# A two-layer conditioned transformer on one core: two orders of work per attention unit, on ScalarE and on VectorE, are swapped

## The chip, the cores and the metric

One Trainium2 chip, of which the kernel uses one core. The metric is the time of one execution on the device in microseconds (us), of which the median over several runs counts. The engines of the core are TensorE (PE in the profile, its weight loads PEld), VectorE (DVE), ScalarE (ACT), GpSimd (POOL) and SyncE (SP), which issues every DMA of this kernel.

## What is computed

Input are 16 sequences of 256 tokens with 512 features, float32. Two transformer layers follow each other:

```
layer 0: h = layernorm(x) * (1 + scale) + shift
         q = h Wq (16 heads of 32), latent = h Wkd, k = latent Wku, v = latent Wvu (4 kv heads)
         rotate q, k;  softmax(q k / sqrt(32), window of 64 and every 64th key, by blocks of 128) v
         x = x + y Wo
layer 1: h = rmsnorm(x) * gain1;  q = h Wq (8 heads of 64), k = h Wk, v = h Wv (one kv head)
         rotate q, k;  softmax(q k / sqrt(64), all 256 keys) v;  x = x + y Wo
         h = rmsnorm(x) * gain2;  x = x + (silu(h Wg) * (h Wu)) Wd        (inner width 2048)
```

The matrix products are made of float16 halves: each operand is a high half (the value rounded to float16) and a low half (the rest), and a product is three matmuls, high by high, high by low and low by high.

## The kernel before, in words

**Rounds.** The 16 sequences go in 8 pairs. The attention of both layers of pair n runs together with the MLP of pair n-1: a round. The first round has no MLP beside it (it prepares the weights instead), seven rounds are a loop with both, and a last MLP stands alone. A table `PLAN` of named steps (`scores0`, `unit0_0` to `unit0_23`, `unit1_0` to `unit1_15` and others) says how many of the MLP's 128 parts, of six 128x512 matmuls each for the first 64, TensorE makes at each step. A chunk of the MLP is four parts: two for the gate bank, two for the up bank.

**Units.** A unit is one PSUM bank of scores: four heads by 128 keys (layer 0, first 128 tokens, units 0 to 7), two heads by 193 keys (layer 0, last 128 tokens, units 8 to 23) or two heads by 256 keys (layer 1, 16 units). For each unit j:

1. TensorE makes the scores (`unit_scores`, L1403 in layer 0, L1407 and L1409 in layer 1). It does so two units ahead (`AHEAD = 2`): at step j it makes the parts of the MLP, the scores of unit j+2, then the values of unit j-4 (`LAG = 4`).
2. VectorE takes the minimum of each head's row (`lows`, L1027 with the mask in layer 0, L1031 in layer 1).
3. ScalarE takes the exponentials in place, a head at a time, with their sums (`exps`, L808).
4. ScalarE writes the float16 high half into `prob` (`prob_highs`, L817). `prob` has three slots, so this waits for the transposition of unit j-3 (`turned_before`), and for the exponentials of its own unit (`terms_made`).
5. VectorE writes the low half (`prob_lows`, L1038). This frees the bank.
6. SyncE transposes both halves by DMA into `prob_t` (`turn_probs`, L563; the fifth place of the ring is named `x_mid` or `q_t`), once the values of unit j-5 are made.
7. TensorE multiplies with v (`unit_values`, L1339 to L1341 with `v_hi`, `v_lo`).

There are four banks for the scores (`BANKS = 4`), used in a fixed order. The scores of unit j+2 wait in `bank_for` for the `prob_lows` of the bank's last user, unit j-2 as a rule.

**What else stands in the units' steps.** ScalarE has two hooks for the MLP: `ahead(step)` makes the tanh of a chunk whose gate products fall in this step (`tanhs`, L970, waits for TensorE), `behind(step)` the high half of a finished chunk (`inner_highs`, L976). VectorE's `between` makes the gate's product (`gates`, L1296, waits for the tanh) and the chunk's inner value (`inners`, L1306). SyncE loads the next weights of the MLP, 512 KB at a time, at the step that finishes a chunk (`ring_loads`, L542), in the one queue that also has the transpositions. Every engine runs its own list in order; only semaphores tie them.

Of the kernel before, what the change touches and what calls it, by code (L numbers as in the profile page):

```python
# [100 lines left out]
def unit_index(layer, j):  # L101
    return layer * UNITS[0] + j
# [87 lines left out]
def chunks_at(step, done):  # L190
    return [f for f in range(FCH) if 4 * f + done - 1 in parts_at(step)]
# [6 lines left out]
def count(n, per, k):  # L198
    i, off = n
    return off * per + k if i is None else i * per + (off * per + k)  # L200


def need(eng, sem, value):
    if isinstance(value, int) and value <= 0:
        return
    eng.wait_ge(sem, value)
# [20 lines left out]
def build(nc, x, cond_t, pos_t, w_ada_t, b_ada_t, wq0_t, wkd_t, wku_t, wvu_t, wo0_t, ln1_w, tw1_t,  # L227
          ln2_w, tw2_t, wq1_t, wk1_t, wv1_t, wo1_t, wg_t, wu_t, wd_t, mask_c, rope0_c, freq_c,
          wgu, out):
    with ExitStack() as ctx:  # L230
# [232 lines left out]
        def terms(ap, layer, j):  # L463
            s, t, columns = UNIT[layer][j]
            if columns[0][2] != K_TWO:
                return ap
            return ap.rearrange("p (h k) -> p h k", k=TOK)[:, :, 0:K_TWO]
# [11 lines left out]
        def turned_before(eng, n, g):  # L479

            if g < SLOTS:
                n, last = (n[0], n[1] - 1), max(k for k in range(sum(UNITS))
                                                if k % SLOTS == g % SLOTS)
            else:
                last = g - SLOTS
            need(eng, prob_in[last % TURNED], turned_count(n, last))
# [288 lines left out]
        def _(act):  # L775
# [18 lines left out]
            def heads(n, layer, s, t):  # L794
                use = USE[f"heads{layer}", s, t]
                need(act, full, count(n, USES, use + 1))
                act.activation(act_t[s][0][:, :, t * P:(t + 1) * P],
                               work_bank[use % BANKS][:].rearrange("p (c q) -> p c q", c=CH),
                               ACT.Copy).then_inc(hi_done, 1)
# [13 lines left out]
            def prob_highs(n, layer, j):  # L813
                g = unit_index(layer, j)
                need(act, terms_made, count(n, sum(UNITS), g + 1))
                turned_before(act, n, g)
                act.activation(terms(prob[:, g % SLOTS, 0, :], layer, j),  # L817
                               terms(work_bank[USE[f"unit{layer}", j] % BANKS][:], layer, j),
                               ACT.Copy).then_inc(hi_done, 1)

            def layers(n, m):
                def ahead(step):
                    if m is not None:
                        tanhs(m, chunks_at(step, 2))
                    else:
                        weight_highs(step)
                        if step == "fill2.0":
                            act.wait_ge(gains_made, 4 * CH)
                    if step == SINES_AT:
                        sines_((n[0], n[1] + 1))  # L830

                def behind(step):
                    if m is not None:
                        inner_highs(m, chunks_at(step, 4))
# [6 lines left out]
                def units(layer):  # L841
                    total = UNITS[layer]
                    ahead(f"scores{layer}")
                    exps(n, layer, 0)
                    behind(f"scores{layer}")
                    for j in range(total):
                        if j + 1 < total:
                            exps(n, layer, j + 1)
                        ahead(f"unit{layer}_{j}")
                        prob_highs(n, layer, j)  # L850
                        if j in FILL_AT[layer]:
                            heads(n, layer, FILL_AT[layer][j], 0)
                        behind(f"unit{layer}_{j}")
# [100 lines left out]
            def weight_highs(step):  # L954
                for piece in PIECES_AT.get(step, ()):
                    act.wait_ge(*landed[PIECE_OF[piece][0]])
                    for src, dst in piece_views(piece, 0):
                        ins = act.activation(dst, src, ACT.Copy, scale=WS)
                    ins.then_inc(raw_high, 1)

            def sines_(n):
                need(act, angle_ready, count(n, 1, 1))
                act.activation(reduced, reduced, ACT.Sin).then_inc(sines, 1)

            def tanhs(n, chunks):
                for f in chunks:
                    need(act, g_full, count(n, FCH, f + 1))
                    if f > 0:
                        need(act, inner_ready, count(n, FCH, f))
                    act.activation(silu[:], gbank[:], ACT.Tanh, scale=0.5 / WS).then_inc(  # L970
                        tanh_done, 1)
# [18 lines left out]
        def _(dve):  # L990
# [44 lines left out]
            def prob_lows(n, layer, j):  # L1035
                name, slot = (f"unit{layer}", j), unit_index(layer, j) % SLOTS
                need(dve, hi_done, count(n, HI_USES, HI_USE[name] + 1))
                dve.tensor_tensor(terms(prob[:, slot, 1, :], layer, j),  # L1038
                                  terms(work_bank[USE[name] % BANKS][:], layer, j),
                                  terms(prob[:, slot, 0, :], layer, j),  # L1040
                                  ALU.subtract).then_inc(prob_split, 1)
# [16 lines left out]
            def units(n, m, layer):  # L1058
                total = UNITS[layer]
                between(m, f"scores{layer}")  # L1060
                lows(n, layer, 0)
                lows(n, layer, 1)
                for j in range(total):
                    step = f"unit{layer}_{j}"
                    between(m, step)
                    if step in LN_STATS:
                        ln_stats((n[0], n[1] + 1), LN_STATS[step])
                    elif step in LN_APPLY:
                        ln_apply((n[0], n[1] + 1), LN_APPLY[step])
                    if j + 2 < total:  # L1070
                        lows(n, layer, j + 2)
                    prob_lows(n, layer, j)
                    if j in FILL_AT[layer]:
                        heads_low(n, layer, FILL_AT[layer][j], 0)
                    if j in NORM_AT[layer]:
                        normalise(n, layer, NORM_AT[layer][j], 0)
# [60 lines left out]
            def ln_apply(n, s):  # L1137
                need(dve, ln_rstd_ready, count(n, 2, s + 1))
                for t in range(TILES):
                    dve.tensor_scalar(normed[s][:, t, :], x_in[:, s, t, :], moments[:, s, t, 0:1],  # L1140
                                      ln_rstd[:, s, t:t + 1], ALU.subtract, ALU.mult).then_inc(
                                          ln_ready, 1)
# [550 lines left out]
```

## Time and profile before

| | |
|---|---|
| median of three runs | 1889.67 us (1888.66 to 1891.92) |
| the profiled execution's own time | 1891.67 us |
| its span | 1889.9 us |
| TensorE busy | 1733.3 us, 92% |
| VectorE busy | 1162.3 us, 61% |
| ScalarE busy | 928.2 us, 49% |
| GpSimd busy | 380.4 us, 20% |
| mean granted TensorE clock | 0.965 of full speed |

A busy time is a union over instructions. Matmuls overlap, so a TensorE that is busy 92% of the span is not one that streams at its peak for 92% of it. The idle time that a view gives before an instruction is the time in which its engine had nothing running, and the releaser is what ended it.

### The profile page before, as it was taken

To read this page: it belongs to the slowest core of one execution; us is meant where nothing else is said; L and a number is where in the kernel's file an instruction comes from. 1 tells how busy PE (TensorE), PEld (TensorE's weight loads), DVE (VectorE), ACT (ScalarE), POOL (GpSimd) and SP (SyncE) were. 2 spreads that over 40 slices of the span, in tenths; PEclk is the share of its full clock that TensorE was granted. 3 is DMA by queue.
4 is the path that set the end of the run, shared out by engine and by line. 5 is a ranking of instruction groups with operands and counts; after the bars stand their busy time and mean duration, and the time that the engine had idled before them with its cause. 6 is when DMAs were issued, how large, how long until landed. Compare 5 with 4: busy or idle time off the path is not lost.

```text
span 1889.9 us, 38576 instructions
## 1 busy us (share of the span) xinstructions
PE 1733.3 (92%) x12496; PEld 953.7 (50%) x12496; DVE 1162.3 (61%) x2960; ACT 928.2 (49%) x2783; POOL 380.4 (20%) x530
## 2 busy tenths in 40 slices
PE   6656799999999999899999999999999999999999
PEld 4533444555455554455445554555545554455444
DVE  5758657574576756676576755766576755767320
ACT  3644537454473546545374545635465444735320
POOL 5847511111110111111111111102111101111120
PEclk9567799999999999999999999999999999999999
DMA  7996439552594527843495616925286535946220
GB/s 241 223 287 181 89 87 182 127 110 77 131 177 93 107 76 167 148 104 73 126 177 121 123 58 140 194 73 101 89 182 132 116 81 126 175 100 118 89 73 23
DMA packets 520638, 240.86 MB, mean 127 GB/s; under 512 B 476368, under 2 KB 485584, under 8 KB 520400
## 3 DMA queue, kind: packets, MB, share of 16 engines
q1 hardware_dynamic: 520400, 238.01, 57.1%
q8 instruction: 110, 1.80, 0.4%
q14 instruction: 128, 1.05, 0.2%
HBM read 96.38 MB, written 16.78 MB: 60 GB/s over the span
## 4 chain that ended last, share of the span: by engine, by line
PE 71%; DMA 10%; DVE 8%; issue 4%; ACT 4%; SPq 2%; DVEq 0%; POOL 0%; ACTq 0%; POOLq 0%
DMA prob_t<-prob 10%; PE up L1339 7%; PE gate L1341 7%; PE gate L1339 7%; PE up L1341 7%; PE gate L1340 7%; PE up L1340 7%; PE bank L1339 4%; PE bank L1340 4%; PE bank L1341 4%; PE y L1339 4%; PE y L1340 3%; PE y L1341 3%; PE bank L1366 2%; ACT bank L808 2%
## 5 line engine op out<-in xcount | busy, mean ns | idle before, releaser
L808 ACT ACTIVATE bank<-bank,low 128x128 f32<-128x128 f32 (+2 forms) x768 | 304.3, 399 | 162.9 <-DVE low L1031 106.0
L680 POOL TENSOR_TENSOR inner_t<-inner,inner_t 128x512 f16<-128x512 f32 x128 | 148.0, 1156 | 792.5 <-ACT inner_t L976 792.5
L1038 DVE TENSOR_TENSOR prob<-bank,prob 128x512 f16<-128x512 f32 (+1 forms) x320 | 203.7, 637 | 100.9 <-ACT prob L817 99.9
L817 ACT ACTIVATE prob<-bank 128x512 f16<-128x512 f32 (+1 forms) x320 | 180.9, 565 | 58.6 <-DMA prob_t<-prob 53.5
L1296 DVE SCALAR_TENSOR_TENSOR silu<-silu,gate 128x512 f32<-128x512 f32 x128 | 87.9, 687 | 186.3 <-ACT silu L970 186.3
L1339 PE MATMUL up<-mlp,ring 128*128 128x512 f16 x512 | 194.5, 380 | 0.7 <-DVE inner L1306 0.7
L1339 PE MATMUL gate<-mlp,ring 128*128 128x512 f16 x512 | 194.1, 379 | 0.4 <-DVE mlp L1007 0.4
L1341 PE MATMUL gate<-mlp,ring 128*128 128x512 f16 x512 | 194.4, 380 | 0.0
L1340 PE MATMUL gate<-mlp,ring 128*128 128x512 f16 x512 | 194.2, 379 | 0.0
L1341 PE MATMUL up<-mlp,ring 128*128 128x512 f16 x512 | 194.2, 379 | 0.0
L1340 PE MATMUL up<-mlp,ring 128*128 128x512 f16 x512 | 194.2, 379 | 0.0
L808 ACT ACTIVATION_READ_ACCUMULATOR bank<-bank,low 128x1 f32 x768 | 160.9, 210 | 0.0
L1027 DVE CUSTOM_DVE_ANT_0 bank<-bank,mask 128x193 f32<-128x193 f32 (+1 forms) x512 | 152.5, 351 | 4.0 <-PE bank L1403 3.9
L1339 PE MATMUL y<-v_hi,prob_t 128*128 128x32 f16 (+2 forms) x1024 | 111.6, 187 | 35.3 <-DMA prob_t<-prob 34.4
L1306 DVE SCALAR_TENSOR_TENSOR inner<-up,silu 128x512 f32<-128x512 f32 x128 | 87.9, 687 | 79.7 <-PE up L1341 79.0
L970 ACT ACTIVATE silu<-gate 128x512 f32<-128x512 f32 x128 | 76.8, 600 | 115.3 <-PE gate L1341 114.3
L951 ACT ACTIVATE work<-x_mid 128x512 f32<-128x512 f32 x64 | 40.3, 630 | 177.1 <-DVE x_mid L1096 177.1
L976 ACT ACTIVATE inner_t<-inner 128x512 f16<-128x512 f32 x128 | 80.7, 630 | 77.9 <-DVE inner L1306 77.9
L1339 PEld LDWEIGHTS y<-v_hi,prob_t 128*128 128x128 f16 (+1 forms) x1024 | 91.2, 99 | 50.1 <-DMA prob_t<-prob 42.8
L1339 PE MATMUL y<-wq_hi,act_hi 128*128 128x512 f16 x256 | 98.2, 384 | 13.5 <-DVE work L1103 12.0
L1340 PE MATMUL y<-v_lo,prob_t 128*128 128x32 f16 (+2 forms) x1024 | 110.2, 185 | 0.0
L1341 PE MATMUL y<-v_hi,prob_t 128*128 128x32 f16 (+2 forms) x1024 | 110.1, 185 | 0.0
(168 smaller groups left out, 4047.2 us busy)
## 6 DMA issues: line engine op xcount, KB each, us to landing
ring<-wgu_dram SPq DMA_DIRECT2D x124, 512.0 KB, 3.9
x_in<-x_dram SPq DMA_DIRECT2D x18, 512.0 KB, 5.4
x_res<-x_mid SPq DMA_DIRECT2D x16, 512.0 KB, 3.0
out_dram<-x_res SPq DMA_DIRECT2D x32, 256.0 KB, 2.3
inner_t<-wg_t_dram SPq DMA_DIRECT2D x8, 512.0 KB, 5.2
inner_t<-wu_t_dram SPq DMA_DIRECT2D x8, 512.0 KB, 5.1
prob_t<-prob SPq DMA_TRANSPOSE x256, 3.3
wgu_dram<-ring SPq DMA_DIRECT2D x8, 512.0 KB, 5.1
```

The source lines that it names most:

```text
L680: pool.tensor_tensor(inner_t[:, 1, f, :], inner[:], inner_t[:, 0, f, :], ALU.subtract).then_inc(inner_low, 1)
L808: ins = act.activation(bank_[:, at:at + wid], bank_[:, at:at + wid], ACT.Exp, bias=low[:, j % BANKS, k:k + 1], scale=-1.0, accum_out=total)
L817: act.activation(terms(prob[:, g % SLOTS, 0, :], layer, j), terms(work_bank[USE[f"unit{layer}", j] % BANKS][:], layer, j), ACT.Copy).then_ ...
L970: act.activation(silu[:], gbank[:], ACT.Tanh, scale=0.5 / WS).then_inc(tanh_done, 1)
L976: act.activation(inner_t[:, 0, f, :], inner[:], ACT.Copy).then_inc(inner_high, 1)
L1027: ins = dve.tensor_tensor_reduce(out=view, in0=view, in1=mask[:, 0:wid], scale=1.0, scalar=3.0e38, op0=ALU.add, op1=ALU.min, accum_out=low ...
L1038: dve.tensor_tensor(terms(prob[:, slot, 1, :], layer, j), terms(work_bank[USE[name] % BANKS][:], layer, j), terms(prob[:, slot, 0, :], lay ...
L1296: dve.scalar_tensor_tensor(silu[:], silu[:], 1.0, gbank[:], ALU.add, ALU.mult).then_inc(gated, 1)
L1306: dve.scalar_tensor_tensor(inner[:], ubank[:], 0.5 * HS / (WS * WS), silu[:], ALU.mult, ALU.mult).then_inc(inner_ready, 1)
L1339: pe.matmul(out_ap, left[0], right[0], start=start, stop=False)
L1340: pe.matmul(out_ap, left[0], right[1], start=False, stop=False)
L1341: return pe.matmul(out_ap, left[1], right[0], start=False, stop=stop)
```

## The change

Two swaps, nothing else. On ScalarE, `prob_highs` of unit j stood behind the exponentials of unit j+1 and the tanh of the step; it now stands ahead of both, and the exponentials stand behind the tanh. On VectorE, `prob_lows` of unit j stood behind `lows` of unit j+2; it now stands ahead.

```diff
@@ units(layer), ScalarE
                     for j in range(total):
+                        prob_highs(n, layer, j)
+                        ahead(f"unit{layer}_{j}")
                         if j + 1 < total:
                             exps(n, layer, j + 1)
-                        ahead(f"unit{layer}_{j}")
-                        prob_highs(n, layer, j)
                         if j in FILL_AT[layer]:
                             heads(n, layer, FILL_AT[layer][j], 0)
                         behind(f"unit{layer}_{j}")
@@ units(n, m, layer), VectorE
+                    prob_lows(n, layer, j)
                     if j + 2 < total:
                         lows(n, layer, j + 2)
-                    prob_lows(n, layer, j)
                     if j in FILL_AT[layer]:
                         heads_low(n, layer, FILL_AT[layer][j], 0)
```

No instruction is added or taken away, and nothing on TensorE, GpSimd or SyncE moves in its own list.

How the instructions stand on ScalarE in the loop, layer 0, from unit 8's exponentials (bank2, 193 columns) on, before:

```order
L808 ACTIVATE bank2,sums0<-bank2,low 128x193 x2
L817 ACTIVATE prob<-bank1 128x512
L206 REGISTER_ALU
L808 ACTIVATE bank3,sums0<-bank3,low 128x193 x2
L206 REGISTER_ALU
L817 ACTIVATE prob<-bank2 128x2x193
L206 REGISTER_ALU
L808 ACTIVATE bank0,sums0<-bank0,low 128x193 x2
L817 ACTIVATE prob<-bank3 128x2x193
L976 ACTIVATE inner_t<-inner 128x512
```

And the same place in the changed kernel:

```order
L808 ACTIVATE bank2,sums0<-bank2,low 128x193 x2
L206 REGISTER_ALU
L817 ACTIVATE prob<-bank2 128x2x193
L206 REGISTER_ALU
L808 ACTIVATE bank3,sums0<-bank3,low 128x193 x2
L817 ACTIVATE prob<-bank3 128x2x193
L206 REGISTER_ALU
L808 ACTIVATE bank0,sums0<-bank0,low 128x193 x2
L976 ACTIVATE inner_t<-inner 128x512
L817 ACTIVATE prob<-bank0 128x2x193
```

Before, a bank's high half comes one unit's exponentials after its own; now it comes right behind them, with only a hook of the MLP (L976) between in some steps.

VectorE at step `unit0_0` of the loop, before (unit 2's minima in bank0, unit 0's low half from bank2):

```order
L1296 SCALAR_TENSOR_TENSOR silu<-silu,gate 128x512
L213 REGISTER_ALU
L1027 ISA bank0,low<-bank0,mask 128x128
L1027 ISA low 128x1
L1027 ISA bank0,low<-bank0,mask 128x128
L1027 ISA low 128x1
L1027 ISA bank0,low<-bank0,mask 128x128
L1027 ISA low 128x1
L1027 ISA bank0,low<-bank0,mask 128x128
L1027 ISA low 128x1
L206 REGISTER_ALU
L1038 TENSOR_TENSOR prob<-bank2,prob 128x512
```

And now:

```order
L1296 SCALAR_TENSOR_TENSOR silu<-silu,gate 128x512
L206 REGISTER_ALU
L1038 TENSOR_TENSOR prob<-bank2,prob 128x512
L213 REGISTER_ALU
L1027 ISA bank0,low<-bank0,mask 128x128
L1027 ISA low 128x1
L1027 ISA bank0,low<-bank0,mask 128x128
L1027 ISA low 128x1
L1027 ISA bank0,low<-bank0,mask 128x128
L1027 ISA low 128x1
L1027 ISA bank0,low<-bank0,mask 128x128
L1027 ISA low 128x1
```

The low half moved in front of the whole of the minima; the gate's product, which waits for the tanh, still stands ahead of both.

## Rows read from the trace of the kernel before

**Rows 1.** The page: busy time by engine, and TensorE in 40 slices

```profile
PE 1733.3 (92%) x12496; PEld 953.7 (50%) x12496; DVE 1162.3 (61%) x2960; ACT 928.2 (49%) x2783; POOL 380.4 (20%) x530
PE   6656799999999999899999999999999999999999
```

**Rows 2.** TensorE's waits, 240 to 1740 us (the seven rounds): us, times, longest

```profile
PE y L1339 <- DMA prob_t<-prob: 22.4, 28, 2.2
PE bank L1403 <- DVE prob L1038: 16.1, 21, 1.2
```

**Rows 3.** TensorE's waits, 0 to 240 us (the first round)

```profile
PE bank L1407 <- DVE prob L1038: 14.9, 9, 2.8
PE y L1339 <- DMA prob_t<-prob: 12.0, 11, 1.9
PE bank L1403 <- DVE prob L1038: 9.3, 13, 0.9
```

**Rows 4.** Timeline of TensorE at three places: start, us, instruction, idle before

```profile
957.76 0.40 PE L1403 MATMUL bank<-k_t,q_t 96*128 96x128 f16 x4 [1.23 <-DVE prob L1038]
...
999.93 0.34 PE L1403 MATMUL bank<-k_t,q_t 96*128 96x193 f16 x2 [0.71 <-DVE prob L1038]
...
1176.22 0.28 PE L1403 MATMUL bank<-k_t,q_t 96*128 96x128 f16 x2 [1.22 <-DVE prob L1038]
```

**Rows 5.** Timeline of VectorE, 955 to 957 us

```profile
955.46 0.69 DVE L1296 SCALAR_TENSOR_TENSOR silu<-silu,gate 128x512 f32<-128x512 f32 x1 [2.30 <-ACT silu L970]
956.06 0.29 DVE L1027 CUSTOM_DVE_ANT_0 bank<-bank,mask 128x128 f32<-128x128 f32 x1
...
957.01 0.69 DVE L1038 TENSOR_TENSOR prob<-bank,prob 128x512 f16<-128x512 f32 x1
```

**Rows 6.** Timeline of ScalarE, 954 to 959 us

```profile
954.82 0.60 ACT L970 ACTIVATE silu<-gate 128x512 f32<-128x512 f32 x1 [1.46 <-PE gate L1341]
955.32 0.59 ACT L817 ACTIVATE prob<-bank 128x512 f16<-128x512 f32 x1
...
957.19 0.34 ACT L808 ACTIVATE bank<-bank,low 128x128 f32<-128x128 f32 x1 [0.76 <-DVE low L1027]
...
957.55 0.33 ACT L808 ACTIVATE bank<-bank,low 128x128 f32<-128x128 f32 x1
...
958.58 0.61 ACT L817 ACTIVATE prob<-bank 128x512 f16<-128x512 f32 x1
```

**Rows 7.** Timeline of VectorE, 969 to 971 and 998 to 1000 us

```profile
969.60 0.36 DVE L1027 CUSTOM_DVE_ANT_0 bank<-bank,mask 128x193 f32<-128x193 f32 x1
...
970.19 0.69 DVE L1038 TENSOR_TENSOR prob<-bank,prob 128x512 f16<-128x512 f32 x1
...
998.72 0.36 DVE L1027 CUSTOM_DVE_ANT_0 bank<-bank,mask 128x193 f32<-128x193 f32 x1
...
999.31 0.56 DVE L1038 TENSOR_TENSOR prob<-bank,prob 128x386 f16<-128x386 f32 x1
```

**Rows 8.** Timeline of SyncE's queue and, last, of TensorE, 969 to 977 us

```profile
969.04 0.45 SPq L542 DMA_DIRECT2D ring<-wgu_dram  x1
970.95 5.20 SPq L563 DMA_TRANSPOSE prob_t<-prob  x3
...
976.07 0.19 PE L1339 MATMUL y<-v_hi,prob_t 128*128 128x32 f16 x1 [1.27 <-DMA prob_t<-prob]
```

**Rows 9.** DMA of one round's layer 0 units, 946 to 1008 us: KB each, median us to landing

```profile
ring<-wgu_dram SPq DMA_DIRECT2D x9, 512.0 KB, 3.9
prob_t<-prob SPq DMA_TRANSPOSE x20, 4.0
```

**Rows 10.** Windows: one layer 0 units' stage, the first round's layer 1 (last: clock, DMA share, GB/s)

```profile
946.00:1008.00 62.00, 56.53 (x520) 30.90 (x519) 44.81 (x173) 45.70 (x171) 11.10 (x10) 1.00 0.95 184
168.00:212.00 44.00, 26.12 (x228) 18.76 (x229) 34.87 (x57) 27.16 (x87) 31.63 (x44) 0.54 0.71 141
```

**Rows 11.** ScalarE's waits, 240 to 1740 us

```profile
ACT silu L970 <- PE gate L1341: 94.9, 42, 5.2
...
ACT prob L817 <- DMA prob_t<-prob: 34.1, 34, 3.6
```

**Rows 12.** VectorE's waits, 168 to 212 us (the first round's layer 1)

```profile
DVE prob L1038 <- ACT prob L817: 4.2, 7, 1.3
```

**Rows 13.** Timeline of VectorE, 978.8 to 980 us (the second waits for the first)

```profile
978.83 0.24 DVE L1082 RECIPROCAL inv<-sums 128x16 f32<-128x16 f32 x1
979.10 0.69 DVE L1084 TENSOR_TENSOR work<-y,inv 128x512 f32<-128x512 f32 x1
979.71 0.68 DVE L1296 SCALAR_TENSOR_TENSOR silu<-silu,gate 128x512 f32<-128x512 f32 x1
```

## The prediction

> **What bounds the kernel now.** I read the page first: TensorE is busy 92% of the span and, once the first round is over at about 240 us, nine tenths or more of nearly every slice [rows 1]. So a change that moves no matmul can win only what TensorE idles. I then asked for TensorE's waits, apart for the seven rounds of the loop and for the first. In the loop two releasers can be touched by this change: a unit's transposition that lands late (22.4 us in 28 waits) and a low half that frees a bank of scores late (16.1 us in 21) [rows 2]. That is 38.5 us in seven rounds, 5.5 us a round. In the first round the same two kinds come to 36.2 us [rows 3], but there ScalarE, VectorE and the DMA queue set the pace and TensorE has little to do, so a wait of TensorE there is a symptom.
>
> The third view is the timeline of the round that ends near 1165 us. There the 1.23 us before the scores at 957.76 end with a low half [rows 4]. That low half, of unit 1, stood behind the masked minima of unit 3: VectorE's minima began at 956.06 and the low half at 957.01 [rows 5]. Its input, the high half, was made at 955.32 to 955.91 [rows 6]. So it could have begun at 956.06.
>
> **The change part by part.** The durations are those of the profiled execution, whose time is 1891.67 us, 2.0 above the median of the three runs; I take the difference from the median.
>
> *The scores' waits.* Three gaps of this kind come back in every round (21 waits in seven rounds). The low half now starts before the minima, so it comes earlier by what the minima take: 0.95 us at the first (956.06 to 957.01) [rows 5], 0.59 at the second (969.60 to 970.19) and 0.59 at the third (998.72 to 999.31) [rows 7]. The first gap is 1.23 us, the third 0.71 [rows 4]; the second must be 16.1 / 7 - 1.23 - 0.71 = 0.36 us, less than its 0.59. I take 0.95 + 0.36 + 0.59 = 1.9 us a round. Bounds: nothing, if each low half now waits for something else, and all 2.3 us.
>
> *The transpositions' waits.* A high half now comes earlier on ScalarE: at the tanh of 954.82 [rows 6] the list was exponentials 2, tanh 1, high 1, and unit 2's high half had to wait for exponentials 3, until 958.58. Now, after the tanh's 0.50 us (954.82 to 955.32), exponentials 2 take four times 0.35 (957.19 to 958.58 for four), and high half 2 follows at about 956.9, or 957.4 with L976 between. So it is 1.2 to 1.7 us earlier, and VectorE's low half follows it without the minima between. The transposition is issued when both are there. How much of that reaches the landing? Transposition 6, which TensorE waited 1.27 us for, was issued at 970.95 and landed at about 976.0: 5.1 us, because a load of 512 KB was issued at 969.04, just ahead of it in the same queue [rows 8]. The load, in turn, had waited on SyncE behind the transposition of unit 5, which waits for that unit's low half. Both move forward, but TensorE moves forward too when the scores' waits go, so a landing must come earlier by that much to keep its gap as it is. I take half of the 22.4 us, 1.6 us a round. Bounds: nothing and 3.2 us.
>
> *Behind the tanh.* The exponentials of unit j+1 now stand behind the tanh of step j, which waits for TensorE's gate products (94.9 us in 42 waits) [rows 11]. They lose the head start they had. I cost this at nothing: a tanh at T leaves high half j+1 done at about T + 0.5 + 1.4 + 0.6 = T + 2.5, where before it was T + 0.5 + 0.6 + 1.4 + 0.6 or later, with exponentials j+2 in front. The cover is that ScalarE has 16.3 us idle in these 62 us and VectorE 17.2 [rows 10]. Minima j+2 come later by a low half, 0.6 us, but exponentials j+2 are not wanted before high half j+1 is done.
>
> *The wait for its own engine.* The high half used to have another unit's exponentials between it and its own, and now waits for the instruction right before it. The nearest row is VectorE's reciprocal, at 978.83 for 0.24 us, with its user starting at 979.10, 0.03 us after the end, where instructions that don't wait start 0.08 us before the end (979.71 after one that ends at 979.79) [rows 13]. So 0.11 us a unit, 40 units a round. In the loop ScalarE's idle time covers it. In the first round's units 0 to 7 ScalarE is the pace, and 8 x 0.11 is 0.9 us; the end of that stretch is set by the transpositions, so I count 0 with a bound of +2. The Trainium skill, VectorE: DVE Perf Modes, section The DRAIN you can't avoid, says that a semaphore after each copy costs nothing extra over a chain without. By it this term would be zero everywhere; rows 13 show a small cost, and the sum is the same by both.
>
> *The first round.* In its layer 0 the transpositions share the queue with the weights' loads; earlier halves change nothing there: 0, bounds -3 and +2. In its layer 1 VectorE is busy 34.9 of 44 us [rows 10] and waits 4.2 us for high halves that stood behind exponentials [rows 12]. I take 3 us of that; bounds 0 and 9, the latter if waits of PE's chain behind it go too.
>
> Sum: 7 x (1.9 + 1.6) = 24.5, plus 3: 27.5 us. 1889.7 - 27.5 is **1862 us**. With all waits of rows 2 gone and the far bounds of the first round it is 38.5 + 9 + 3 = 50.5, 1839 us.
>
> **The rivals.**
>
> *A. The DMA queue is already the limit in layer 0's units.* For: the DMA engines' share is 0.95 over 62 us [rows 10], and a transposition takes 4.0 us to land at the median there [rows 9]. Then the order of the engines is of no use beyond the earlier start. Each round would win about the first 0.95 us, the first round 3: 1889.7 - 6.7 - 3 = 1880 us. Against: SyncE issues three transpositions in 5.2 us right behind a load [rows 8], 1.7 us each, against some 2.6 us a unit in the stage (62 us / 24), and with 9 loads in the stage there is a little room. The Trainium skill, DMA: Bandwidth & Descriptors, section Latency and other measured facts, gives 261 GB/s as the effective rate of one transposing kernel; 256 KB of `prob` are an estimated 1.0 us by it. The stage moves 184 GB/s [rows 10], so by that page too rival A would be the less likely.
>
> *B. The tanh behind the high half (slower).* The high half j waits for the transposition of unit j-3 (34.1 us in 34 waits, 3.6 the longest, in the loop) [rows 11], and the tanh of step j is now behind it. The gate bank then is free late, and TensorE's next gate products wait. TensorE has 12 up matmuls of about 0.22 us in between, 2.6 us; tanh and gate product take 0.60 + 0.69 [rows 5, 6]. So it decides from a wait of 1.3 us on. If all 34.1 us fell before a tanh that TensorE needs, and only the 1.9 us a round were won, it would be 34.1 - 13.3 = +21: 1911 us. Against: the tanh stands in one step of three or so, most of these waits are under 1.3 us (mean 1.0), and a tanh that does not wait comes earlier by up to a unit's exponentials.
>
> *C. Nothing (same).* The waits for transpositions grow by what the waits for banks shrink, since both lists are tied to TensorE through gate and scores: within 3.8 us of 1889.7, say 1888.
>
> **How the numbers follow.** My forecast has 0.52, rival A 0.24, C 0.13, B 0.11. A measurement of this kernel tells about 0.2% (3.8 us) from no change. A's 1880 is faster by more than that; a small part of it may end within. So faster 0.76, within 0.2% 0.13, slower 0.11. The range goes down to 1843, near the far bound of the sum, and up to 1889, which takes in A and part of C, and leaves out B.
>
> **What would show it.** In the changed profile the three waits of TensorE's L1403 for VectorE's L1038 in each round should be two, shorter ones or none, near 3 us in total in place of 16.1; its waits for transpositions should be about 11 us in the loop. ScalarE's idle time before L817 should end with DMA oftener than now, and VectorE's wait for L817 in the first round's layer 1 should fall from 4.2 to about 1 us. A round, now 218.5 us from this wait to the same wait of the next (957.76 to 1176.22) [rows 4], should be about 215. I am wrong if TensorE waits for `silu` at gate products (B), if its waits for transpositions stay at 22 us or grow (A, C), or if the busy time of any engine changes.

## The result, and the profile after

The changed kernel takes **1873.16 us**, the median of four runs (1872.47 to 1873.19), against 1890.67 us for four runs of the kernel before (1888.66 to 1891.92). The ratio is 0.9907, 95% interval 0.9891 to 0.9922: 17.5 us faster, where 27.5 were forecast. The profiled execution took 1873.14 us, its span is 1871.3, and I compare it with the span of 1889.9 before: 18.6 us.

Where did they come from? The starts of the rounds, taken at the same instruction of ScalarE in the two traces, stand 2.5 us earlier at the end of the first round and 16.2 us earlier six rounds later, where the eighth round begins; the span is 18.6 us shorter. So a round is about 2.3 us shorter (13.7 us in six), and all behind the first round, the last MLP included, 16.1.

The page of the changed kernel, beside [rows 1]. Of the 18.6 us, 13.6 are less idle time of TensorE (156.6 us before, 143.0 now) and 5.0 less busy time, which no view explains:

```profile
PE 1728.3 (92%) x12496; PEld 951.8 (51%) x12496; DVE 1157.8 (62%) x2960; ACT 944.5 (50%) x2783; POOL 381.1 (20%) x530
PE   6656799999989999899999999999999999999999
```

TensorE's waits from 240 to 1740 us, beside [rows 2] (us, times, longest):

```profile
PE y L1339 <- DMA prob_t<-prob: 11.5, 16, 1.3
PE y L1339 <- DVE work L1084: 9.3, 14, 0.7
PE bank L1403 <- issue: 8.2, 7, 1.5
PE bank L1403 <- DVE prob L1038: 6.2, 14, 0.7
PE up L1339 <- DVE inner L1306: 6.1, 9, 0.8
```

The two waits that the change was aimed at fell from 22.4 and 16.1 us to 11.5 and 6.2: 20.8 us. But two others grew, which I had not named: the wait for the normalised rows (L1084) was 3.8 us in 7 waits before and is 9.3 in 14, the wait of the `up` product for the MLP's inner (L1306) was 0.7 in 2 and is 6.1 in 9. They give 10.9 us back. With the issue wait (9.6 before) these waits shrink by 11.3 us. All idle time of TensorE from 240 to 1740 us fell by 12.1 us (1432.6 us busy of 1500 before, 1444.7 now), so next to nothing of the gain lies in idle times that this view leaves out; what is missing to the 16.1 us is busy time.

In the first round, 0 to 240 us, beside [rows 3]:

```profile
PE bank L1407 <- DVE prob L1038: 13.0, 8, 2.8
PE y L1339 <- DMA prob_t<-prob: 11.6, 11, 1.7
PE bank L1403 <- DVE prob L1038: 9.9, 13, 1.4
```

The timeline of TensorE in one round (start, us, instruction, idle before), beside [rows 4]. The first place has 0.27 us where it had 1.23, the second none, the third (here in the round after) still 0.72. New are the gaps before `up` and before the value products at 966.86 and 969.52:

```profile
946.80 0.40 PE L1403 MATMUL bank<-k_t,q_t 96*128 96x128 f16 x4 [0.27 <-DVE prob L1038]
...
952.34 0.39 PE L1339 MATMUL up<-mlp,ring 128*128 128x512 f16 x1 [0.74 <-DVE inner L1306]
...
966.86 0.19 PE L1339 MATMUL y<-v_hi,prob_t 128*128 128x32 f16 x1 [0.93 <-DMA prob_t<-prob]
...
969.52 0.19 PE L1339 MATMUL y<-v_hi,prob_t 128*128 128x32 f16 x1 [0.73 <-DVE work L1084]
...
1203.68 0.34 PE L1403 MATMUL bank<-k_t,q_t 96*128 96x193 f16 x2 [0.72 <-DVE prob L1038]
```

Who made `up` wait at 952.34? VectorE's inner L1306, whose bank `up` needs. Here is VectorE's list up to it, changed and then before:

```profile
945.46 0.69 DVE L1296 SCALAR_TENSOR_TENSOR silu<-silu,gate 128x512 f32<-128x512 f32 x1 [1.47 <-ACT silu L970]
...
950.04 0.69 DVE L1038 TENSOR_TENSOR prob<-bank,prob 128x512 f16<-128x512 f32 x1 [0.48 <-ACT prob L817]
950.64 0.29 DVE L1027 CUSTOM_DVE_ANT_0 bank<-bank,mask 128x128 f32<-128x128 f32 x1
...
951.60 0.69 DVE L1306 SCALAR_TENSOR_TENSOR inner<-up,silu 128x512 f32<-128x512 f32 x1
```

```profile
959.22 0.69 DVE L1038 TENSOR_TENSOR prob<-bank,prob 128x512 f16<-128x512 f32 x1 [0.51 <-ACT prob L817]
...
961.10 0.69 DVE L1038 TENSOR_TENSOR prob<-bank,prob 128x512 f16<-128x512 f32 x1 [0.18 <-ACT prob L817]
961.71 0.68 DVE L1306 SCALAR_TENSOR_TENSOR inner<-up,silu 128x512 f32<-128x512 f32 x1
```

VectorE waited for high halves in this stretch before as well (0.51 and 0.18 us), so the low half's wait of 0.48 us is not new. What changed is how the engines stand to each other. Against the kernel before, the gate's product starts 10.00 us earlier (955.46, now 945.46), the scores of the first place 10.96 (957.76, now 946.80), and the inner 10.11 (961.71, now 951.60). Between the gate's product and the inner VectorE has the same work in either order: the low halves come sooner, the minima later, the inner hardly moves. So TensorE, let go 0.96 us sooner at the scores, comes to `up` before the inner is made and starts it 10.11 us earlier (962.45 before). It keeps 0.11 us of the 0.96. These steps are the same within 0.02 us in all seven rounds, and in a second profile of the changed kernel.

At 969.52 TensorE waits for the normalised rows. VectorE and ScalarE around it, now:

```profile
967.42 0.56 DVE L1038 TENSOR_TENSOR prob<-bank,prob 128x386 f16<-128x386 f32 x1 [1.85 <-ACT prob L817]
...
968.77 0.69 DVE L1084 TENSOR_TENSOR work<-y,inv 128x512 f32<-128x512 f32 x1
```

```profile
966.89 0.50 ACT L817 ACTIVATE prob<-bank 128x386 f16<-128x386 f32 x1 [1.46 <-DMA prob_t<-prob]
```

Read upwards: the value product waits for the rows of 968.77, these stand behind a low half that waited 1.85 us for a high half, and that one had waited 1.46 us for a transposition to read a `prob` buffer. Such a chain was there before, too, one low half sooner in the list:

```profile
976.64 0.56 DVE L1038 TENSOR_TENSOR prob<-bank,prob 128x386 f16<-128x386 f32 x1 [1.83 <-ACT prob L817]
```

The rows came at 979.10 then [rows 13], and TensorE hardly waited for them (0.07 us, at 979.85). They now come 10.33 us earlier. TensorE was further ahead than that at the product before (977.85, now 966.86: 10.99 us), so it had to wait.

The third place of [rows 4], on VectorE, beside the last pair of [rows 7]:

```profile
1201.40 0.56 DVE L1038 TENSOR_TENSOR prob<-bank,prob 128x386 f16<-128x386 f32 x1
...
1202.46 0.69 DVE L1306 SCALAR_TENSOR_TENSOR inner<-up,silu 128x512 f32<-128x512 f32 x1
1203.07 0.56 DVE L1038 TENSOR_TENSOR prob<-bank,prob 128x386 f16<-128x386 f32 x1
```

The minima are gone from right ahead of this low half, but the inner stands there (before, it stood ahead of the minima), and its high half was itself only done at 1202.82. Of the 0.59 us counted for this place, some 0.1 came (0.61 us mean of seven gaps now, 0.70 before).

The stage of the layer 0 units and the DMA issues in it, 934 to 996 us, beside [rows 9, 10]:

```profile
934.00:996.00 62.00, 58.43 (x531) 32.01 (x531) 46.03 (x176) 48.13 (x174) 11.57 (x10) 1.00 0.95 192
```

```profile
prob_t<-prob SPq DMA_TRANSPOSE x20, 3.4
```

TensorE is busy 58.4 us of 62 where it was 56.5, at the same DMA share of 0.95 (57.1 us at 0.98 in the second profile, 930 to 992 us). So the share was no wall. That transpositions land sooner is not shown: the median of these 20 is 3.4 us where it was 4.0, but 3.8 in the second profile, and over the 224 of the loop it is 3.3 us where it was 3.2.

ScalarE's and VectorE's waits that answer to [rows 11] and [rows 12], the loop and then the first round's layer 1:

```profile
ACT silu L970 <- PE gate L1341: 110.3, 56, 5.2
...
ACT prob L817 <- DMA prob_t<-prob: 42.3, 31, 4.3
```

```profile
DVE prob L1038 <- ACT prob L817: 1.1, 1, 1.1
```

### The profile page after: what moved, and what is told of

It reads as the page before. It is cut to its first block, busy times and chain, and to the rows that moved or that the text cites. A ratio compares the mean times of both kernels' runs of the same rounds, so it can differ in the third digit from the quotient of the medians.

```text
span 1871.3 us, 38576 instructions
## 1 busy us (share of the span) xinstructions
PE 1728.3 (92%) x12496; PEld 951.8 (51%) x12496; DVE 1157.8 (62%) x2960; ACT 944.5 (50%) x2783; POOL 381.1 (20%) x530
## 4 chain that ended last, share of the span: by engine, by line
PE 71%; DMA 9%; DVE 8%; ACT 5%; issue 4%; SPq 2%; DVEq 0%; POOL 0%; ACTq 0%; POOLq 0%
DMA prob_t<-prob 8%; PE gate L1341 7%; PE gate L1339 7%; PE gate L1340 7%; PE up L1339 7%; PE up L1341 7%; PE up L1340 7%; PE bank L1339 4%; PE bank L1340 4%; PE bank L1341 4%; PE y L1339 4%; PE y L1341 4%; PE y L1340 4%; ACT bank L808 3%; PE bank L1366 2%
## 5 line engine op out<-in xcount | busy, mean ns | idle before, releaser
L1306 DVE SCALAR_TENSOR_TENSOR inner<-up,silu 128x512 f32<-128x512 f32 x128 | 88.1, 689 | 82.2 <-PE up L1341 75.1
L976 ACT ACTIVATE inner_t<-inner 128x512 f16<-128x512 f32 x128 | 81.2, 634 | 77.9 <-DVE inner L1306 77.9
L1339 PE MATMUL y<-wq_hi,act_hi 128*128 128x512 f16 x256 | 98.7, 386 | 11.3 <-DVE work L1103 10.3
```

The costliest lines, as they stand in the source:

```text
L976: act.activation(inner_t[:, 0, f, :], inner[:], ACT.Copy).then_inc(inner_high, 1)
L1306: dve.scalar_tensor_tensor(inner[:], ubank[:], 0.5 * HS / (WS * WS), silu[:], ALU.mult, ALU.mult).then_inc(inner_ready, 1)
L1339: pe.matmul(out_ap, left[0], right[0], start=start, stop=False)
```

## The experiments

**Theory:** each half of the change takes away what it was meant to, and the size is cut by other feeds of TensorE that VectorE makes no sooner than before. **Rivals:** the place of the tanh is what matters, in either direction (B); the DMA queue is the limit (A); one of the two swaps does it all. The kernel before took 1893.5 to 1895.8 us at the median beside these runs, and 1890.67 in the first comparison, so each run is given as a ratio to the kernel before beside it, on the same chip. A wait is read from one profile of each run.

### One swap at a time

`act_only`: the changed kernel with VectorE's list as before.

```diff
-                    prob_lows(n, layer, j)
                     if j + 2 < total:
                         lows(n, layer, j + 2)
+                    prob_lows(n, layer, j)
```

> The swap on ScalarE alone, VectorE in its old order. Theory (each swap has its own part): the low half is made behind the minima as before, so TensorE's waits for banks (L1403 for L1038, 16.1 us before and 6.2 in the changed kernel, 240 to 1740 us) stay at 12 to 16 us, while its waits for transpositions (22.4 before, 11.5 changed) fall most of the way; time about 1880 us. Rival (ScalarE's swap is all of it): 1873 us as the changed kernel, and bank waits near 6 us.

Measured: 1887.74 us, ratio 0.9965 (0.9951 to 0.998). In the loop TensorE's waits are

```profile
PE bank L1403 <- DVE prob L1038: 19.0, 28, 1.2
PE y L1339 <- DMA prob_t<-prob: 17.4, 23, 1.7
...
PE y L1339 <- DVE work L1084: 3.8, 7, 0.5
```

`dve_only`: ScalarE's list as before, VectorE's as changed.

```diff
-                        prob_highs(n, layer, j)
-                        ahead(f"unit{layer}_{j}")
                         if j + 1 < total:
                             exps(n, layer, j + 1)
+                        ahead(f"unit{layer}_{j}")
+                        prob_highs(n, layer, j)
```

> The swap on VectorE alone, ScalarE in its old order. Theory (the two swaps need each other): low half j now waits in front of minima j+2, while high half j still stands behind exponentials j+1, and exponentials j+2 need minima j+2; ScalarE and VectorE take turns. A 193-column unit then takes 0.8 (exponentials) + 0.42 (high) + 0.5 (low) + 0.65 (minima) + about 0.2 = 2.6 us against some 2.0 that TensorE needs, a 256-column unit 0.9 + 0.5 + 0.6 + 0.6 + 0.2 = 2.8 against 2.3: over 7 rounds 16 x 0.6 x 7 + 16 x 0.5 x 7 = 120 us more, about 2010 us (1930 to 2090). Rival (each swap has its own part): the bank waits go and it is 1880 us.

Measured: 2089.53 us, ratio 1.1042 (1.101 to 1.1075): 195 us more, where the sum said 120. In the loop, first VectorE's wait, then ScalarE's:

```profile
DVE prob L1038 <- ACT prob L817: 204.8, 167, 2.1
```

```profile
ACT bank L808 <- DVE low L1027: 173.8, 138, 1.8
```

What follows: the halves don't add up. Alone, ScalarE's swap wins over a third of the gain (0.35%). TensorE's waits for transpositions fall by 5 us, but those for the scores' banks rise from 16.1 to 19.0, and the wait for L1084 (3.8) stays; of the 4.3 us by which its span is shorter than that of the kernel before, 3.0 lie in the first round. VectorE's swap alone costs 10%: its minima for unit j+2 stand behind low half j, which waits for a high half that stands behind exponentials j+1, so the two engines take turns (204.8 and 173.8 us, where the kernel before has 72.7 and 54.8). Some 54 of the 198 us by which its span is longer are busy time of TensorE (1786.9 us), whose granted clock was 0.97 to 0.98 in the loop and not 0.99 to 1.00; the sum had no entry for that. Only with the high half moved does the low half have an input when its turn comes. The scores' waits fall below 16.1 us only when both halves are there; those for L1084 rise with VectorE's half (11.8 us in `dve_only`).

### The place of the tanh

`tanh_behind` puts the tanh (the `ahead` hook) behind the exponentials, `tanh_first` ahead of the high half, and `old_tanh_first` gives the old order of both engines with the tanh ahead of the exponentials (its diff is against the kernel before).

```diff
                         prob_highs(n, layer, j)
-                        ahead(f"unit{layer}_{j}")
                         if j + 1 < total:
                             exps(n, layer, j + 1)
+                        ahead(f"unit{layer}_{j}")
```

> The changed kernel with the tanh back behind the exponentials of unit j+1 (high j, exponentials j+1, tanh, high of the inner value). Theory (the early high half makes the gain, the tanh's place little): within 4 us of the changed kernel's 1873. Rival (the gain came from the earlier tanh, by which VectorE's gate product and all behind it are earlier): the tanh is 0.8 to 1.4 us later in every step that has one, low halves behind the gate product too, and half of the gain or more is gone: 1882 us or over.

Measured: 1898.21 us, ratio 1.002 (1.0005 to 1.0035). The whole gain is gone, and the theory with it. VectorE waits 183.0 us for the tanh in the loop in place of 139.6, and ScalarE 58.3 us for the masked minima in place of 10.8. TensorE's waits for transpositions are even shorter (8.0 us), but:

```profile
PE bank L1403 <- DVE prob L1038: 15.5, 21, 1.3
PE y L1339 <- DVE work L1084: 12.9, 14, 1.1
```

```diff
-                        prob_highs(n, layer, j)
                         ahead(f"unit{layer}_{j}")
+                        prob_highs(n, layer, j)
                         if j + 1 < total:
                             exps(n, layer, j + 1)
```

> The changed kernel with the tanh ahead of the high half (tanh j, high j, exponentials j+1), VectorE in the new order. Theory (the high half must not wait for TensorE): in the steps with a tanh the high half waits for the gate products, some 2 us on average in 56 waits, and the waits for transpositions rise again from 11.5 to 15 to 20 us in the loop; 4 to 10 us slower than the changed kernel beside it. Rival (what matters is only that the tanh is ahead of the exponentials): within 3 us of it.

Measured: 1882.23 us, ratio 0.9945 (0.9922 to 0.9969), some 8 us slower than the change. The waits for transpositions stayed at 11.6 us, so the cause that was expected isn't it. Its profile shows the inner's waits at 9.5 us (6.1 and 7.4 in two profiles of the changed kernel), a first round at least 4 us longer than theirs, and some 5 us or more behind it. What makes them is open.

```diff
+                        ahead(f"unit{layer}_{j}")
                         if j + 1 < total:
                             exps(n, layer, j + 1)
-                        ahead(f"unit{layer}_{j}")
                         prob_highs(n, layer, j)
```

> The kernel before with one edit: the tanh moved ahead of the exponentials of unit j+1 (tanh j, exponentials j+1, high j), VectorE in its old order. It asks whether the tanh's earlier place alone makes the gain, since with the tanh behind the exponentials the changed order had none. Theory (tanh and high half must both be ahead): the tanh waits for TensorE before the exponentials are begun, and the high half comes behind both, 0.8 to 1.4 us later than before wherever the tanh waits for TensorE; ratio 1.00 to 1.02. Rival (it is the tanh's place alone): ratio 0.990 to 0.994.

Measured: 1901.15 us, ratio 1.0041 (1.002 to 1.0063); one of the ten executions took 6222.86 us, the others 1896.92 to 1906.74. The tanh's earlier place alone wins nothing; the scores' waits rise to 25.2 us. Together: the swap pays only with the tanh ahead of the exponentials, and the tanh there does not pay without the swap.

### The change once more, and its first round

`changed_again` is the changed kernel unchanged, to see what of the profile comes back.

> The changed kernel once more, as the reference for the runs beside it on the same chip: ratio to the kernel before 0.991, as first measured.

Measured: 1874.55 us, ratio 0.9903 (0.9881 to 0.9925); waits for transpositions 11.1, L1084 9.3, inner 7.4, scores 6.5 us. Behind the first round it is 14.4 us shorter than the kernel before (16.1 in the first profile). In the first profile the last exponential of the first round's layer 0 had come 3.5 us later than before (at 124.0 us, not 120.5); here it comes at 120.1. But here that layer's first exponential had come at 57.3 us, where it came at 61.5 in the other two. From first to last exponential the layer takes 62.8 us, and 62.5 in the first profile, against 59.1 before.

`first_old` gives ScalarE, `first_both_old` both engines, the old order in the first round's layer 0 alone.

```diff
+                        if m is None and layer == 0:
+                            if j + 1 < total:
+                                exps(n, layer, j + 1)
+                            ahead(f"unit{layer}_{j}")
+                            prob_highs(n, layer, j)
+                        else:
...
```

> The changed kernel with ScalarE's old order in the first round's layer 0 alone. Between the first round's start and the end of its layer 0 the changed kernel is 3.5 us behind. Theory (ScalarE sets the pace there and pays for waiting on its own exponentials, 0.13 us a unit, and starts in later DMA slots): those 3.5 us come back, 1870 us. Rival (it is how the DMA queue falls, VectorE's order or chance): 1873 us, and the layer still ends some 3 us late.

Measured: 1882.95 us, ratio 0.9943 (0.9924 to 0.9962). The scores' waits of the first round rise to 28.9 us from 9.9. This was a badly made experiment: it left VectorE's new order there, and so shows the coupling of `dve_only` again and nothing of what was asked.

VectorE's part of `first_both_old` (ScalarE's is that of `first_old`):

```diff
+                    old = m is None and layer == 0
+                    if not old:
+                        prob_lows(n, layer, j)
                     if j + 2 < total:
                         lows(n, layer, j + 2)
+                    if old:
+                        prob_lows(n, layer, j)
```

> The changed kernel with the old order of both engines in the first round's layer 0. The run with ScalarE's alone had VectorE's new order beside it there, and TensorE's waits for banks in that stage rose from 9.9 to 28.9 us. Theory: with both old, the 3.5 us by which the changed kernel is late at the end of that layer come back, and 2 to 4 us of the time. Rival (chance of the DMA queue): no difference beyond 1 us.

Measured: 1873.91 us, ratio 0.9906 (0.9876 to 0.9936). Against 1874.55 of the change on the same chip it is no difference. But the interval is 0.3% to either side, some 6 us, and the effect asked for was 2 to 4. In its profile the layer's first exponential comes at 57.7 us and the last at 120.0, 62.3 us with the old order. So the layer ends at 120.0 to 120.1 with either order when it begins at 57 to 58 us, and at 120.5 with the old and 124.0 with the new when it begins at 61.5. Whether the order costs anything there is open.

### What holds back the rest

Four runs on the 10.9 us of new waits, and on the transpositions' 11.5 us. `norm_first`:

```diff
+                    if j in NORM_AT[layer]:
+                        normalise(n, layer, NORM_AT[layer][j], 0)
                     if j + 2 < total:
                         lows(n, layer, j + 2)
...
-                    if j in NORM_AT[layer]:
-                        normalise(n, layer, NORM_AT[layer][j], 0)
```

> The changed kernel with the normalising of attention rows (DVE L1084) put between a unit's low half and the minima of the unit two ahead. Theory (half of what the swap won is given back because VectorE's other work in the unit now stands behind the minima, which wait for newer scores): TensorE's waits for L1084 in 240 to 1740 us fall from 9.3 us to under 4, some other wait grows by at most 2, loop 3 to 6 us shorter than the changed kernel's, ratio to the kernel before 0.986 to 0.989. Rival (the waits named there only take the place of one another, TensorE is held by the sum of the feeds): L1084 falls, L1403 or the inner L1306 rises by as much, ratio 0.990 to 0.992.

Measured: 1880.51 us, ratio 0.9914 (0.99 to 0.9928).

```profile
PE y L1339 <- DMA prob_t<-prob: 17.4, 20, 1.6
...
PE y L1339 <- DVE work L1084: 2.7, 5, 0.5
```

The wait for L1084 fell by 6.6 us as the theory had it, but TensorE's waits for transpositions rose by 5.9. It was the rival that held, though by another wait than the one it named. In the profile a round is 0.5 to 0.7 us longer than in the two of the changed kernel, and the first round 5 to 7 us, so half or more of what it is slower by lies in the first round; in time, the interval takes in the change's 0.9907. `inner_first`:

```diff
                         prob_highs(n, layer, j)
                         ahead(f"unit{layer}_{j}")
+                        behind(f"unit{layer}_{j}")
                         if j + 1 < total:
                             exps(n, layer, j + 1)
...
-                        behind(f"unit{layer}_{j}")
```

> The changed kernel with the inner highs (the hook behind each unit on ScalarE) put ahead of the next unit's exponentials, as the tanh is. Theory (the new waits of the up product for the inner, 6 to 7 us in 240 to 1740, come from the inner's turn on the two engines): these waits fall to under 3, and the exponentials come about 0.4 us later in the units that carry an inner; ratio 0.987 to 0.990. Rival (the inner's low part on VectorE is what is late, since L1306 is VectorE's and stands behind a low half that itself waits for ScalarE): the waits stay at 6 or grow, and the bank's waits grow too, ratio 0.990 to 0.995.

Measured: 1882.27 us, ratio 0.9924 (0.9911 to 0.9937). The inner's waits are 6.2 us, unmoved: they are made on VectorE, as the rival said, and as the starts at 951.60 and 961.71 above show. Putting the inner ahead of the minima on VectorE, which stand right before it now, was not tried. The scores' waits hardly grew (6.9, against 6.2 and 6.5); those for transpositions did, to 14.4. `norm_inner` has both edits.

> Both of the two edits above at once. Theory: the two gains add up, waits for L1084 and L1306 both under 4 us in 240 to 1740, ratio 0.983 to 0.988. Rival (one limit behind both): no better than the better of the two, ratio 0.989 to 0.995.

Measured: 1880.76 us, ratio 0.9917 (0.9899 to 0.9934). No better than either; waits for transpositions 16.3 us, L1084 3.2, inner 6.6. `load_after`:

```diff
-                    ring_loads(m, step, False)
                     turn(n, step)
+                    ring_loads(m, step, False)
```

> The changed kernel with SyncE's ring loads of a step issued behind that step's transposition instead of ahead of it. Theory (the 11 us that TensorE still waits for transpositions are transfers that share the queues with a step's weight loads): DMA waits in 240 to 1740 fall from 11 to 3 to 8 us, and some matmuls wait for weights for 0 to 4 us; ratio 0.985 to 0.990. Rival A of the prediction (the DMA queues are full whatever the order): the waits only move, DMA as a whole 10 to 14 us, ratio 0.990 to 0.993.

Measured: 1892.56 us, ratio 0.9981 (0.997 to 0.9991), nearly the whole gain lost, against both expectations.

```profile
PE y L1339 <- DMA prob_t<-prob: 21.3, 13, 2.9
PE up L1339 <- DVE inner L1306: 16.6, 16, 1.5
```

Fewer waits for transpositions, but longer ones. All that a round is longer by, 2.8 us, lies between the first and the last exponential of layer 0 (59.0 us mean, 56.0 in the changed kernel). SyncE's queue there shows what the load's old place gave. First the changed kernel, then this one:

```profile
956.17 1.23 SPq L563 DMA_TRANSPOSE prob_t<-prob  x1
957.57 0.46 SPq L542 DMA_DIRECT2D ring<-wgu_dram  x1
960.25 5.22 SPq L563 DMA_TRANSPOSE prob_t<-prob  x3
```

```profile
959.47 1.24 SPq L563 DMA_TRANSPOSE prob_t<-prob  x1
960.87 0.45 SPq L542 DMA_DIRECT2D ring<-wgu_dram  x1
961.60 5.22 SPq L563 DMA_TRANSPOSE prob_t<-prob  x2
```

In the changed kernel the load at 957.57 goes out in the 2.7 us in which SyncE has no transposition to issue, and three transpositions follow together. With the load behind its step's transposition, a load (960.87) is issued between transpositions that are ready. ScalarE then waits longer for `prob` buffers: 50.6 us for `prob_t` transpositions in the loop, against 44.8 in `changed_again`, and 20.2 against 7.2 for those into `x_mid`. So a transposition that lands late does not only hold TensorE; through the buffer it delays high half, low half and all behind them.

In `norm_first` and `norm_inner` a wait of TensorE is taken away (L1084) and returns at the next feed (the transpositions). I read it as a ring: a unit's buffer is free when its transposition has landed, the next high half waits for that, its low half for the high half, its transposition for both. A fourth `prob` buffer, which would open this ring, was not tried. That the ring is what limits the stage is thus argued from the waits, not shown. None of the orders tried is faster than the change beyond its interval; `first_both_old`, `norm_first`, `norm_inner` and, just, `inner_first` can't be told from it.

## Why the prediction was right, and where its size was off

The likeliest case came, faster by more than 0.2%, inside the range, at 17.5 us where 27.5 stood. The two waits fell for the reasons given, by nearly the 24.5 us of the sum (20.8), but half of that was given back by feeds that the sum left out.

- *The scores' waits*, 1.9 us a round by the sum: 16.1 to 6.2 us is 1.4. At the first place the gap went from 1.23 to 0.27 us, the 0.95 counted, of which 0.11 was left at the next `up`; the second, 0.36, is gone; the third gave some 0.1 of its 0.59. The step that failed at the third was to take the minima as all that stood ahead of the low half: in the new list the inner L1306 is right in front of it, and its own high half is late. The text looked for near 3 us in total and a round of 215; they are 6.2 us and 216.4.
- *The transpositions' waits*, 1.6 us a round: 22.4 to 11.5 us is 1.56. "Half" was a guess, and it came to half. `act_only` shows 5 of these 10.9 us as coming with ScalarE's half.
- *TensorE's other feeds* were missing. The sum made no entry for feeds that VectorE makes no sooner while TensorE comes sooner: 5.5 us more for L1084 and 5.4 for the inner, 1.6 us a round. For the inner it is shown to the hundredth: of the 0.96 us won at the scores 0.85 are lost again at `up`, in each of seven rounds. This is the term by which the loop's 24.5 us became 16: 20.8 of the two waits, less 10.9, with 1.4 from the issue wait and some 4 in TensorE's busy time. `norm_first` shows that it isn't a cost with a cure of its own: with its wait gone, that for transpositions is 17.4 again. The text had named the mechanism ("TensorE moves forward too") for one kind of wait only.
- *Behind the tanh*, cost 0: TensorE does not wait for `silu` at gate products among its larger waits. That the idle time of both engines was the cover is not shown. The part hides a term as large as the whole gain: `tanh_behind` keeps the swap with exponentials ahead of the tanh, and is 1.1% slower (1.002 against 0.9907). The sum had no entry for what the tanh's earlier place gives, and that it was not missed is in part luck.
- *The wait for its own engine*, 0.11 us a unit: 0.13 to 0.14 measured on ScalarE, below, which the loop covers. The Trainium skill's VectorE: DVE Perf Modes, section The DRAIN you can't avoid, by which the term would be zero, speaks of copies on VectorE; on ScalarE no run shows it at zero.
- *The first round*, 3 us: 2.5 in the first profile, 5.3 in `changed_again`. In layer 1 VectorE's wait for the high half went from 4.2 to 1.1 us as expected, and from first to last exponential the layer takes 34.7 us in both, 36.8 before. Layer 0, put at 0 with a bound of +2, took 3.4 to 3.7 us longer, with the cause open.
- *The signs of being wrong* had "if the busy time of any engine changes", and it did: ScalarE's from 928.2 to 944.5 us, TensorE's from 1733.3 to 1728.3. The sign was a bad one. Busy time is a union, and the high half no longer overlaps the instruction ahead of it, as the last section shows; the instructions are the same.
- *Rival A* gave a round some 0.95 us and waits that stay at 22 us; a round won 2.3, and the waits halved at a DMA share as high as before. *Rival B*'s wait did grow, ScalarE's for a buffer from 34.1 to 42.3 us (in 31 waits, not 34: longer, not oftener as the text had it), without reaching the gate products. *Rival C* was wrong for the two waits it spoke of and half right in kind: what shrinks in one place grows in another, but by 10.9 of 20.8 us.

## What to carry to other kernels

When a step is moved ahead on an in-order engine, list all that is now behind it, and ask what it waits for: in `dve_only` a low half that waits drags the minima behind it along. And follow the engine that is let go sooner to its next feed: if that one is made no sooner, the time is lost again there (0.85 of 0.96 us here). Swaps on two engines that hand work to each other are to be judged as a pair: here one alone won 0.35%, the other alone cost 10%, both together won 0.9%. So take the sum of all waits of the engine that bounds the kernel, not the two that the change aims at. To see where time is won and lost, compare the start of the same instruction in both traces, engine by engine.

## What the runs showed of the hardware

ScalarE's wait for its own last result can be read where it sets the pace, in the first round. The high halves' starts, before and then after:

```profile
75.89 0.62 ACT L817 ACTIVATE prob<-bank 128x512 f16<-128x512 f32 x1
...
77.69 0.22 ACT L808 ACTIVATION_READ_ACCUMULATOR bank<-bank,low 128x1 f32 x1
77.78 0.62 ACT L817 ACTIVATE prob<-bank 128x512 f16<-128x512 f32 x1
```

```profile
76.06 0.60 ACT L817 ACTIVATE prob<-bank 128x512 f16<-128x512 f32 x1
...
77.83 0.23 ACT L808 ACTIVATION_READ_ACCUMULATOR bank<-bank,low 128x1 f32 x1
78.09 0.60 ACT L817 ACTIVATE prob<-bank 128x512 f16<-128x512 f32 x1
```

A unit of the same instructions (four exponentials, each with its accumulator read, and one high half) takes 1.89 us when the high half reads the exponentials of the unit before, and 2.03 when it reads those right ahead of it: 0.14 us here and 0.13 in the unit after, for a wait on the engine itself. Before, the high half starts 0.13 us ahead of the end of the accumulator read (77.69 and 0.22, then 77.78); now it starts 0.03 behind it (77.83 and 0.23, then 78.09). I had estimated 0.11 from VectorE.

Two figures of this case are weaker than they look. The median of 20 transpositions from issue to landing in one stage was 4.0, 3.4 and 3.8 us in three profiles, while that of the loop's 224 was 3.2 before and 3.3 after. And a DMA share of 0.95 over 62 us did not keep a round from getting 2.3 us shorter by a change of order alone.
